# Two gated attention and expert layers: layer 1's values reach their rows through DRAM, probabilities lie by key and then head, layer 0's values are made a step sooner

## The chip, the cores and the metric

One core of a Trainium2 chip runs the whole program. The metric is the time on the device in microseconds; the times are medians of several runs. The engines are PE (TensorE, products and transposes), DVE (VectorE), ACT (ScalarE), POOL (GpSimd) and SP (SyncE, which here only issues transfers). Each engine works through its own list of instructions in order and waits on semaphores.

## What is computed

32 sequences of 128 tokens of width 128, with a context of 77 keys each, go through two layers. Layer 0 attends with 8 heads of 64, layer 1 with 16 heads of 8. After each attention stand 8 experts, of which each token takes two.

```
x = x + tanh(g_xattn[0]) * xattn0(layernorm(x), ctx)      # 8 heads of 64
x = x + tanh(g_ffn[0])   * experts0(layernorm(x))         # top 2 of 8
x = x + tanh(g_xattn[1]) * xattn1(layernorm(x), ctx, ctx) # 16 heads of 8
x = x + tanh(g_ffn[1])   * experts1(layernorm(x))
# xattn1: q = x@Wq+bq; k = ctx@Wk+bk; v = ctx@Wv+bv, by head
#         softmax(q k^T / sqrt(8)) v, then @Wo + bo
```

All of it is float32. Where more accuracy is needed than one rounded product gives, an operand is split into a rounded high part and the rest, and three products are added ("three passes").

## The kernel before

`order` writes out by hand one list of tasks, the plan, by generators for four phases: attention 0 (57 to 278 us of the trace), experts 0, attention 1 (462 to 740 us), experts 1. Every engine walks the same plan and does its part of each task, so the plan sets the order on each queue. A **split task** (`ctx`, `xt`, `q1`, `k1`, `k0` and so on) is a product on PE into a PSUM bank, a rounded copy on ACT and the rest on DVE (L1170, or L1168 with a bias). `bank_of` gives each task its bank. In layer 1 all splits and `v1` use `SPLIT_BANK`, number 5, and so do that layer's routing tasks (`mturn`, `route`, `rank`, `totals`), which pick the experts; a task waits until the one before it in the bank has been read (`bank_free`). Bank 6, `V_BANK`, takes layer 0's values and, in layer 1, the turned values of `rows1`.

Attention works on **units** of 8 heads x 77 keys = 616 columns of scores for 128 tokens. Layer 0 has one unit for a sequence, layer 1 two: 64 units, 8 for a **group** of four sequences. For each unit PE makes the scores (L759, L774), DVE takes the maximum by head (L1154) and subtracts it (L1157) from PSUM into `prob`, ACT takes the exponential, PE turns the 616 columns in five chunks of up to 128 (L782), ACT copies them to `prob_t` (L1082), and PE multiplies them with the values (L801 in layer 0, L816 in layer 1), whose rows must lie as the columns did: by head, then key. In layer 0 DVE also sums each head (L1208) and POOL divides (L1498).

Layer 0's values are made for a sequence in two halves (`v0`, PE L695 to L697, ACT L1069), written to DRAM (SP L624) and read back with the right rows (`v0_load`, SP L630 and L631). They are made in step u for sequence u, loaded in step u + 1, and used by `weigh0` in step u + 2.

Layer 1's values come from `v1`, once for a group: three passes of 308 columns, with the feature on the partition; ACT copies them repeated (L1089, tile `v_t`). `rows1`, twice for each sequence, turns five windows of them on PE (L879, 160 in all), ACT copies these to `v_raw` (L1098, 64 copies), and POOL multiplies with the mask `row_head`, so that each row keeps its own head's 8 columns (L1549, 128 operations, into `v_flat`). Each chunk of `weigh1` reads 108 columns, more than the 72 that it needs. Here the profile writes `v_raw` for `v1_raw`, `v_flat` for `v1_flat` or `v1_rows`, `v_t` for `v1_t`, and `o_both` for `o_sb`.

`up_raw` is the staging tile by which the layer 1 keys and queries go to DRAM (SP L638, L641) and come back stacked (SP L658 with 12 issues for a group, L663).

## Time and profile before

| | us |
|---|---|
| median of 3 runs | 917.65 |
| lowest, highest | 908.68, 921.89 |
| the profiled execution, its own time | 926.61 |
| its span | 924.7 |

| engine | busy us | share of the span |
|---|---|---|
| PE | 725.0 | 78% |
| DVE | 556.2 | 60% |
| POOL | 507.0 | 55% |
| ACT | 458.2 | 50% |

The mean granted TensorE clock is 0.888 of full speed. The span leaves 1.9 us of the profiled time outside, and the profiled execution is 9.0 us longer than the median. Busy shares are means over phases that differ, so each phase has to be read by itself: which engine is nearly full there, and what its idle time waits for.

### The profile page before, as it was taken

To read this page: it belongs to the slowest core of one execution; us is meant where nothing else is said; L and a number is where in the kernel's file an instruction comes from. 1 tells how busy PE (TensorE), PEld (TensorE's weight loads), DVE (VectorE), ACT (ScalarE), POOL (GpSimd) and SP (SyncE) were. 2 spreads that over 40 slices of the span, in tenths; PEclk is the share of its full clock that TensorE was granted. 3 is DMA by queue.
4 is the path that set the end of the run, shared out by engine and by line. 5 is a ranking of instruction groups with operands and counts; after the bars stand their busy time and mean duration, and the time that the engine had idled before them with its cause. 6 is when DMAs were issued, how large, how long until landed. Compare 5 with 4: busy or idle time off the path is not lost.

```text
span 924.7 us, 17016 instructions
## 1 busy us (share of the span) xinstructions
PE 725.0 (78%) x4514; PEld 626.1 (68%) x4514; DVE 556.2 (60%) x1933; ACT 458.2 (50%) x1207; POOL 507.0 (55%) x734
## 2 busy tenths in 40 slices
PE   5677988887879769897867888888788886677870
PEld 3466777777767557786756777777677776676760
DVE  2356777887755546575656767767767634334554
ACT  2355755665534324344455656556466543354441
POOL 4113667675676657556453327547547655655553
PEclk9988997997987979998979989889899977799895
DMA  9225445333342223243523323313313022323444
GB/s 256 100 73 153 144 143 153 117 116 116 115 141 62 72 80 108 73 117 103 150 54 89 99 66 100 99 48 101 113 48 96 30 69 68 95 77 99 127 131 148
DMA packets 131004, 95.91 MB, mean 104 GB/s; under 512 B 30512, under 2 KB 119120, under 8 KB 130848
## 3 DMA queue, kind: packets, MB, share of 16 engines
q1 hardware_dynamic: 118976, 73.89, 29.6%
q0 software_dynamic: 9088, 19.68, 6.0%
q10 hardware_dynamic: 2848, 1.26, 0.5%
q8 instruction: 40, 0.66, 0.3%
q14 instruction: 52, 0.43, 0.2%
HBM read 55.10 MB, written 44.10 MB: 107 GB/s over the span
## 4 chain that ended last, share of the span: by engine, by line
PE 41%; issue 16%; DVE 15%; ACT 10%; POOL 6%; SPq 5%; DMA 4%; another core or an unknown queue 2%; DVEq 0%; POOLq 0%; ACTq 0%
PE banks L816 5%; PE banks L985 5%; POOL y_rows L1594 3%; PE banks L695 3%; PE banks L969 3%; PE banks L960 3%; PE banks L782 2%; PE banks L801 2%; DVE row_max L1154 2%; PE banks L958 2%; PE banks L697 2%; PE banks L959 2%; PE banks L696 2%; PE banks L937 2%
## 5 line engine op out<-in xcount | busy, mean ns | idle before, releaser
L1594 POOL DMA_INDIRECT y_rows<-y_sb,result_at x156 | 151.2, 969 | 128.1 <-DVE y_sb L1408 54.2
L1587 POOL DMA_INDIRECT x_rows<-xm,row x128 | 128.2, 1002 | 40.1 <-issue 30.8
L985 PE MATMUL banks<-down,hidden_t 128*128 x624 | 108.6, 302 | 0.1
L969 PE MATMUL banks<-ident,hidden 128*128 128x128 f32 x312 | 67.1, 300 | 47.9 <-ACT hidden_t L1134 30.3
L1382 DVE TENSOR_TENSOR xb_l<-banks,xb_h 128x128 fp32r<-128x128 f32 x156 | 45.2, 290 | 90.4 <-ACT xb_h L1120 61.1
L816 PE MATMUL banks<-v_flat,prob_t 128*128 128x108 f32 (+2 forms) x640 | 92.6, 298 | 7.0 <-POOL v_flat L1549 5.4
L816 PEld LDWEIGHTS banks<-v_flat,prob_t 128*128 128x128 f32 (+1 forms) x640 | 88.0, 213 | 13.4 <-ACT prob_t L1082 8.2
L1082 ACT ACTIVATE prob_t<-banks 128x512 f32<-128x512 f32 x192 | 73.2, 436 | 41.5 <-PE banks L782 40.6
L985 PEld LDWEIGHTS banks<-down,hidden_t 128*128 128x128 f32 x624 | 92.9, 214 | 0.6 <-issue 0.3
L1549 POOL TENSOR_TENSOR v_flat<-v_raw,row_head 104x64 f32<-104x64 f32 (+1 forms) x128 | 56.2, 464 | 65.2 <-ACT v_raw L1098 64.5
L1154 DVE TENSOR_REDUCE row_max<-banks 128x8 f32<-128x616 f32 x96 | 75.8, 789 | 25.9 <-PE banks L774 19.5
L969 PEld LDWEIGHTS banks<-ident,hidden 128*128 128x128 f32 x312 | 40.6, 150 | 68.3 <-issue 38.0
L1498 POOL TENSOR_TENSOR prob<-prob,inv_sum 128x616 f32<-128x616 f32 x32 | 39.0, 1220 | 58.5 <-DVE inv_sum L1211 58.4
L1134 ACT ACTIVATE hidden_t<-banks 128x256 f32<-128x256 f32 x156 | 59.3, 380 | 20.4 <-remote 10.1
L1126 ACT ACTIVATE gate<-banks 128x256 f32<-128x256 f32 x78 | 29.9, 384 | 79.5 <-PE banks L960 59.6
L1129 ACT ACTIVATE hidden<-banks 128x256 f32<-128x256 f32 x78 | 30.1, 386 | 69.2 <-PE banks L960 40.5
L937 PE MATMUL banks<-ident,x_norm 128*128 128x128 f32 x156 | 48.7, 312 | 18.1 <-DMA x_norm<-x_rows 11.0
L1157 DVE TENSOR_TENSOR prob<-banks,row_max 128x616 f32<-128x616 f32 x75 | 60.0, 800 | 2.6
L801 PE MATMUL banks<-vo_flat,prob_t 128*128 128x128 f32 (+1 forms) x320 | 49.0, 309 | 13.1 <-issue 10.2
L782 PE MATMUL banks<-ident,prob 128*128 128x128 f32 (+1 forms) x375 | 57.5, 288 | 0.0
L1394 DVE TENSOR_TENSOR hidden<-banks,gate 128x256 f32<-128x256 f32 x78 | 32.9, 422 | 40.8 <-ACT gate L1126 22.3
L801 PEld LDWEIGHTS banks<-vo_flat,prob_t 128*128 128x128 f32 (+1 forms) x320 | 46.8, 224 | 14.2 <-issue 11.2
(221 smaller groups left out, 1934.9 us busy)
## 6 DMA issues: line engine op xcount, KB each, us to landing
x_norm<-x_rows SPq DMA_DIRECT2D x156, 72.0 KB
v_rows<-vo SPq DMA_DIRECT2D x64, 154.0 KB
vo_flat<-v_rows SPq DMA_DIRECT2D x32, 256.0 KB
gathered<-y_rows SPq DMA_DIRECT2D x48, 128.0 KB
q_rows<-up_raw SPq DMA_DIRECT2D x8, 512.0 KB
q_even<-q_rows SPq DMA_DIRECT2D x12, 256.0 KB
q_odd<-q_rows SPq DMA_DIRECT2D x12, 256.0 KB
y_rows<-y_sb,result_at POOLq DMA_INDIRECT x156
```

What stands on the lines that cost most here:

```text
L782: done = pe.transpose(banks[0:chunk_rows[c], PT_BANK[k], c % 4 * SEQ:(c % 4 + 1) * SEQ], flat[:, c * P:c * P + chunk_rows[c]], ident[:, :])
L801: done = pe.matmul(banks[:, O_BANK, 0:D], prob_t[0:rows, b % 2, c, :], vo_flat[0:rows, b % 2, c, :], start=c == 0, stop=c == CHUNKS - 1)
L816: done = pe.matmul(banks[:, O_BANK, half * width:half * width + cols], prob_t[0:rows, u % 2, c, :], v1_flat[0:rows, first:first + cols], s ...
L937: pe.transpose(banks[:, X_BANK, 0:P], x_in[:, i % XR, 0:D], ident[:, :]).then_inc(sem("x_turned"))
L969: done = pe.transpose(banks[:, HT_BANK, half * P:(half + 1) * P], hidden[:, i % 2, half * P:(half + 1) * P], ident[:, :])
L985: done = pe.matmul(banks[:, Y_BANK[i % 2], 0:D], hidden_t[:, i % 2, half, :], of_expert(flat[:, (2 * layer + half) * D:], i, D), start=hal ...
L1082: act.activation(dst, banks[0:rows, PT_BANK[k], 0:len(chunks) * SEQ], ACT.Copy).then_inc(sem("prob_t"))
L1134: act.activation(hidden_t[:, i % 2, :, :].rearrange("p t n -> p (t n)"), banks[:, HT_BANK, 0:HID1], ACT.Copy).then_inc(sem("hidden_t"))
L1154: dve.tensor_reduce(m_view, s_view, AX.X, ALU.max).then_inc(sem("row_max"))
L1157: dve.tensor_tensor(prob_view.rearrange("p (k s) n -> p k s n", k=2), s_view, m_view.unsqueeze(3).to_broadcast([P, 2, 4, NKEY]), ALU.subtr ...
L1587: pool.indirect_dma_start(out=x_rows[i // HG][:, :], out_offset=bass.IndirectOffsetOnAxis(ap=row[:, n, c:c + 1], axis=0), in_=xm[:, i % 2, ...
L1594: pool.indirect_dma_start(out=y_rows[k][:, :], out_offset=bass.IndirectOffsetOnAxis(ap=result_at[:, i % (2 * YR):i % (2 * YR) + 1], axis=0 ...
```

## The change

- **Probabilities by key, then head.** `prob` is laid out [77, 8] and no longer [8, 77]. DVE's subtraction reads the scores in PSUM with a step of 77 elements (four heads in the innermost dimension, then the other bank, then the key); the sum by head in layer 0 reads with a step of 8 elements; POOL's division and the exponential read as they lie. A chunk of 128 columns is now 16 keys x 8 heads, except the last, of 13 keys. Layer 0's values are written to DRAM in that order, so a transfer's runs are 2 KB and no longer 512 bytes.
- **Layer 1's values through DRAM.** `v1` has the key on the partition: 4 sequences x three passes of 77 x 128. DVE adds the bias into `up_raw`, after a wait for the keys' transfers out of it; SP writes it to DRAM (`v1_nat`, tile `v_nat` in the rows). A new task `v_load`, for two sequences, reads five chunks back, each key's row repeated on 8 partitions. `rows1` is now POOL alone: two operations of 128 x 320 for a sequence. The mask is the same for all chunks, [128, 8], and is made from the identity by DVE. The 160 transposes, the 64 copies and the repeated copy are gone. `weigh1` reads 72 columns in every chunk.
- **The freed bank.** From group 2 on, `xt`, `k1`, `q1` and `v1` of layer 1 use bank 6; the routing tasks keep bank 5.
- **Layer 0's values a step sooner.** `v0` for sequence u + 1 and `v0_load` for sequence u stand in step u.

```diff
@@ attention0_steps
-        if 0 <= u - 1 < NSEQ:
-            step.append(("v0_load", u - 1))
+        if u == 0:
+            step += [("v0", 0, 0), ("v0", 0, 1)]
         if 0 <= u - 2 < NSEQ:
             step.append(("weigh0", u - 2))
         if u < NSEQ:
-            step += [("v0", u, 0), ("divide0", u)] + more[1]
+            step.append(("v0_load", u))
+        if u + 1 < NSEQ:
+            step.append(("v0", u + 1, 0))
...
@@ attention1_steps
+            if u % 2 == 1:
+                step.append(("rows1", u // 2))
+            if u and u % 4 == 0:
+                step.append(("v_load", u // 4))
@@ prepare_attention1
-    return out + [("norm", n), ("k1", g), ("normalize", n), ("k_load", g), ("xt", n), ("q1", g), ("q_load", g)]
+    out += [("norm", n), ("k1", g), ("normalize", n), ("k_load", g), ("v1", g), ("xt", n), ("q1", g), ("q_load", g)]
+    return out + ([("v_load", 0)] if g == 0 else [])
@@ bank_of
+        if t[0] == "xt" and t[1] >= NG + 2 or t[0] in ("k1", "q1", "v1") and t[1] >= 2:
+            return V_BANK
@@ sync
+                elif t[0] == "v_load":
+                    q = t[1]
+                    w.wait_ge("v1_ones", 6)
+                    w.wait_ge("v1_staged", 16 * (q // 2 + 1))
+                    w.wait_ge("v1", 4 * q)
...
+                    for c in range(CHUNKS):
+                        rows = chunk_rows[c]
+                        sync.dma_start(v1_raw[0:rows, c, :, :].rearrange("p t d -> p (t d)"),
+                                       src[c * KEYS:c * KEYS + rows // UH, :].unsqueeze(1).to_broadcast([rows // UH, UH, 2 * D])).then_inc(sem("v1_in"), 16)
@@ tensor, v1
+                    for j in range(GS):
+                        c0 = g * GK + j * NKEY
+                        done = three_pass(banks[0:NKEY, bank, j * D:(j + 1) * D], ctx_th[:, c0:c0 + NKEY], ctx_tl[:, c0:c0 + NKEY],
+                                          w1_h[:, 2, :], w1_l[:, 2, :])
@@ vector, soften
-                dve.tensor_tensor(prob_view.rearrange("p (k s) n -> p k s n", k=2), s_view,
-                                  m_view.unsqueeze(3).to_broadcast([P, 2, 4, NKEY]), ALU.subtract).then_inc(sem("shifted"))
+                dve.tensor_tensor(prob_view.rearrange("p n (k s) -> p n k s", k=2), s_view.rearrange("p k s n -> p n k s"),
+                                  m_view.unsqueeze(1).to_broadcast([P, NKEY, 2, 4]), ALU.subtract).then_inc(sem("shifted"))
@@ vector, v1
+                    w.wait_ge("k_staged", 16 * HEAD_SETS * (g + 1))
+                    w.wait_ge("q_staged", 16 * g)
+                    dve.tensor_tensor(up_raw[0:NKEY, 0, :].rearrange("n (j d) -> n j d", d=D),
+                                      banks[0:NKEY, bank_of(t), :].rearrange("n (j d) -> n j d", d=D),
+                                      bv1[0:NKEY, :].unsqueeze(1).to_broadcast([NKEY, GS, D]), ALU.add).then_inc(sem("v1_nat"))
@@ gpsimd, rows1
+                    w.wait_ge("v1_in", 16 * CHUNKS * (b // 2 + 1))
+                    w.wait_ge("pv", NSEQ + 2 * (b - 1))
                     for half in (0, 1):
+                        pool.tensor_tensor(v1_rows[:, b % 2, half, :, :, 0:DK1],
+                                           v1_raw[:, :, b % 2 * 2 + half, :].rearrange("p c (h d) -> p c h d", d=DK1),
+                                           row_head[:, :].unsqueeze(1).unsqueeze(3).to_broadcast([P, CHUNKS, UH, DK1]), ALU.mult).then_inc(sem("v1"))
```

PE in attention 1, in the unit in which the routing's `rank` stands (`picked,earlier` to `picked,ones`); `x_norm` is the transpose of `xt`, `v_t` that of `rows1`. Before:

```order
L816 MATMUL banks<-v_flat,prob_t 128x108 x5
L879 MATMUL banks<-ident,v_t 128x128 x4
L782 MATMUL banks<-ident,prob_extra 128x128 x4
L782 MATMUL banks<-ident,prob_extra 104x128
L730 MATMUL banks<-ident,x_norm 128x128 x4
L879 MATMUL banks<-ident,v_t 104x128
L886 MATMUL banks<-ident,o_both 128x128
L920 MATMUL banks<-picked,earlier 128x32
L921 MATMUL banks<-counts,ones 128x32
L923 MATMUL banks<-picked,ones 128x24
```

And in the changed kernel, from the last three of the twelve passes of `v1`:

```order
L722 MATMUL banks<-w_h,ctx_th 77x128
L723 MATMUL banks<-w_h,ctx_tl 77x128
L724 MATMUL banks<-w_l,ctx_th 77x128
L914 MATMUL banks<-ident,o_both 128x128
L948 MATMUL banks<-picked,earlier 128x32
L949 MATMUL banks<-counts,ones 128x32
L951 MATMUL banks<-picked,ones 128x24
L951 MATMUL banks<-picked,ones 128x16
L951 MATMUL banks<-picked,ones 128x8
L807 MATMUL banks<-k_even,q_even 128x308 x2
L848 MATMUL banks<-v_flat,prob_t 128x72 x5
```

Before, `xt` stands ahead of `rank` in bank 5; now `v1` stands there, in bank 6, and `xt` comes a unit later.

SP in attention 1, the transfers of a group. Before:

```order
L658 DMA k_even<-k_rows 8x16x77 [waits k_staged,scores]
L658 DMA k_even<-k_rows 8x16x77 x11
L671 DMA gathered<-y_rows 128x256 [waits combined]
L641 DMA q_rows<-up_raw 128x2x512 [waits q_stack,split_lo]
L663 DMA q_even<-q_rows 32x4x512 [waits q_staged]
L663 DMA q_even<-q_rows 32x4x512 x2
```

In the changed kernel:

```order
L685 DMA k_even<-k_rows 8x16x77 [waits k_staged,scores]
L685 DMA k_even<-k_rows 8x16x77 x11
L658 DMA v_nat<-up_raw 77x512 [waits v1_nat]
L698 DMA gathered<-y_rows 128x256 [waits combined]
L667 DMA v_raw<-v_nat 128x1x256 [waits v1]
L667 DMA v_raw<-v_nat 128x1x256 x3
L667 DMA v_raw<-v_nat 104x1x256
L653 DMA q_rows<-up_raw 128x2x512 [waits q_stack,split_lo]
```

The write of the values and one of the group's two loads (five issues) stand between the keys' loads and the queries' write; the load waits for POOL (`v1`).

PE in attention 0, its first steps: the scores of sequence 0 (`k_t,xt_h`), then keys (`wqk`) and values (`wvo`). Before:

```order
L759 MATMUL banks<-k_t,xt_h 128x308 x4
L759 MATMUL banks<-k_t,xt_l 128x308 x2
L695 MATMUL banks<-ctx_th,wqk_h 128x308
L696 MATMUL banks<-ctx_th,wqk_l 128x308
L697 MATMUL banks<-ctx_tl,wqk_h 128x308
L695 MATMUL banks<-wvo_h,ctx_th 77x512
L696 MATMUL banks<-wvo_h,ctx_tl 77x512
L697 MATMUL banks<-wvo_l,ctx_th 77x512
L695 MATMUL banks<-ctx_th,wqk_h 128x308
```

In the changed kernel:

```order
L792 MATMUL banks<-k_t,xt_l 128x308 x2
L722 MATMUL banks<-ctx_th,wqk_h 128x308
L723 MATMUL banks<-ctx_th,wqk_l 128x308
L724 MATMUL banks<-ctx_tl,wqk_h 128x308
L722 MATMUL banks<-wvo_h,ctx_th 77x512
L723 MATMUL banks<-wvo_h,ctx_tl 77x512
L724 MATMUL banks<-wvo_l,ctx_th 77x512
L722 MATMUL banks<-wvo_h,ctx_th 77x512
L723 MATMUL banks<-wvo_h,ctx_tl 77x512
L724 MATMUL banks<-wvo_l,ctx_th 77x512
L722 MATMUL banks<-wvo_h,ctx_th 77x512
```

Both halves of sequence 0 and the first of sequence 1 now follow the first keys; from there on every pair of halves is one sequence ahead.

## Rows read from the trace of the kernel before

**Rows 1.** The page's first line.

```profile
span 924.7 us, 17016 instructions
```

**Rows 2.** Busy time in three stretches; columns as in its first line.

```profile
core 0: us, PE busy (x) PEld busy (x) DVE busy (x) ACT busy (x) POOL busy (x), PEclk, DMA share, GB/s
57.00:278.00 221.00, 183.25 (x1121) 157.80 (x1121) 159.09 (x509) 124.85 (x276) 135.54 (x178) 0.89 0.45 129
462.00:740.00 278.00, 226.62 (x1564) 201.69 (x1562) 190.46 (x603) 163.54 (x391) 146.05 (x252) 0.90 0.29 79
180.00:210.00 30.00, 24.15 (x165) 20.43 (x163) 25.31 (x87) 18.94 (x42) 20.99 (x29) 1.00 0.41 120
```

**Rows 3.** Waits of PE in 462:740: waited for, us in total, times, longest us.

```profile
PE banks L920 <- DVE xt_l L1170: 10.4, 5, 2.5
PE banks L695 <- ACT v_t L1089: 5.6, 6, 1.1
PE banks L816 <- POOL v_flat L1549: 5.4, 5, 3.0
PE banks L899 <- DVE up_raw L1168: 5.3, 5, 1.1
...
PE banks L879 <- ACT v_raw L1098: 3.0, 4, 1.8
```

**Rows 4.** Timeline, PE: start us, us, engine, line, tiles, count, [idle before <- releaser].

```profile
573.29 1.23 PE L816 MATMUL banks<-v_flat,prob_t 128*128 128x108 f32 x10
...
578.57 0.27 PE L886 MATMUL banks<-ident,o_both 128*128 128x128 f32 x1
581.30 0.26 PE L920 MATMUL banks<-picked,earlier 128*128 128x32 f32 x1 [2.45 <-DVE xt_l L1170]
...
582.60 2.24 PE L816 MATMUL banks<-v_flat,prob_t 128*128 128x108 f32 x10
```

**Rows 5.** Chain of waits, 560:606, in order of time: start us, us, what.

```profile
577.21 0.44 PE banks L879 x4
...
601.54 0.41 PE banks L695
601.95 0.14 PE banks L696
```

**Rows 6.** Groups by line and shape: busy us, mean ns, idle before, releasers.

```profile
L1549 POOL TENSOR_TENSOR v_flat<-v_raw,row_head 128x256 f32<-128x256 f32 x64 | 39.0, 632 | 56.4 <-ACT v_raw L1098 56.1
...
L1549 POOL TENSOR_TENSOR v_flat<-v_raw,row_head 104x64 f32<-104x64 f32 x64 | 17.7, 296 | 8.8 <-ACT v_raw L1098 8.3
...
L1098 ACT ACTIVATE v_raw<-banks 128x512 f32<-128x512 f32 x64 | 28.2, 441 | 45.4 <-PE banks L879 41.0 <-issue 4.3
```

**Rows 7.** DVE by line and shape: busy us, mean ns, idle before, releasers.

```profile
L1157 DVE TENSOR_TENSOR prob<-banks,row_max 128x616 f32<-128x616 f32 x75 | 60.0, 800 | 2.6
...
L1208 DVE TENSOR_REDUCE row_sum<-prob 128x8 f32<-128x616 f32 x32 | 25.4, 792 | 5.2 <-ACT prob L1064 2.4 <-issue 0.5
...
L1170 DVE TENSOR_TENSOR xt_l<-banks,xt_h 128x512 fp32r<-128x512 f32 x16 | 11.0, 690 | 9.6 <-ACT xt_h L1026 8.6 <-issue 1.0
...
L1319 DVE TENSOR_REDUCE row_f<-rank_hot 128x8 f32<-128x64 f32 x16 | 3.5, 220 | 0.5
L1302 DVE TENSOR_REDUCE group_sum<-picked 128x8 f32<-128x32 f32 x16 | 3.4, 209 | 0.5
```

**Rows 8.** Waits of PE in 57:280.

```profile
PE banks L801 <- issue: 10.2, 3, 5.3
...
PE banks L801 <- DMA vo_flat<-v_rows: 2.8, 1, 2.8
```

**Rows 9.** Timeline, 216:232: the load of layer 0's values and its product.

```profile
222.18 0.53 SPq L630 DMA_DIRECT2D vo_flat<-v_rows  x1
...
225.38 1.35 PE L801 MATMUL banks<-vo_flat,prob_t 128*128 128x128 f32 x10 [3.52 <-issue]
```

**Rows 10.** Timeline, SP's queue: the twelve issues of a group's keys.

```profile
571.57 8.33 SPq L658 DMA_DIRECT2D k_even<-k_rows  x12
```

More of the change, by code:

```diff
@@ L51 @@
 CHUNKS = (UNIT_ROWS + P - 1) // P
+FULL = CHUNKS - 1
+KEYS = P // UH
 chunk_rows = [min(P, UNIT_ROWS - c * P) for c in range(CHUNKS)]
-chunk_key = [c * P % NKEY for c in range(CHUNKS)]
 CHUNK_SETS = (range(0, 4), range(4, CHUNKS))
-V1_WINDOW = 108
-REP = max(k + n for k, n in zip(chunk_key, chunk_rows))
-REP_COPIES = (REP + NKEY - 1) // NKEY
 U1 = 2 * NSEQ
@@ L118, in attention0_steps @@
         if u < NSEQ:
-            step += [("v0", u, 0), ("divide0", u)] + more[1]
+            step.append(("v0_load", u))
+        if u + 1 < NSEQ:
+            step.append(("v0", u + 1, 0))
+        if u < NSEQ:
+            step += [("divide0", u)] + more[1]
         if 0 <= u - 1 < NSEQ:
@@ L122, in attention0_steps @@
         if u < NSEQ:
-            step += [("v0", u, 1), ("bias0", u)] + more[2]
+            step += ([("v0", u + 1, 1)] if u + 1 < NSEQ else []) + [("bias0", u)] + more[2]
         step += more[3] + tasks.get(u, [])
@@ L144, in attention1_steps @@
             step.append(("weigh1", u - 3))
-        if u < U1 and u % per == 0:
-            step.append(("v1", u // per))
-        if u < U1 and u % 2:
-            step.append(("rows1", u // 2, 0))
         if 0 <= u - 2 < U1:
@@ L154, in attention1_steps @@
             pending = pending[n:]
-            step.append(("rows1", u // 2, 1) if u % 2 else ("bias1", u // 2))
+            if u % 2 == 0:
+                step.append(("bias1", u // 2))
+            if u % 2 == 1:
+                step.append(("rows1", u // 2))
+            if u and u % 4 == 0:
+                step.append(("v_load", u // 4))
         if 0 <= u - 4 < U1 and u % 2:
@@ L313, in flamingo_two_layers @@
     v_rows = [nc.dram_tensor(f"v_rows{i}", [UNIT_ROWS, D], F32, kind="Internal").ap() for i in (0, 1)]
+    v1_nat = [nc.dram_tensor(f"v1_nat{i}", [NKEY, GS, D], F32, kind="Internal").ap() for i in (0, 1)]
     q_rows = [nc.dram_tensor(f"q_rows{i}", [2, P, GT], F32, kind="Internal").ap() for i in (0, 1)]
@@ L557, in _ @@
                 load(raw1[:, i * D:(i + 1) * D], a[f"L1_xattn_{name}"], "w_layer1")
[L558 to L559 removed]
+            for i, name in enumerate(("bq", "bk")):
+                load(bqk1[:, i:i + 1], a[f"L1_xattn_{name}"].rearrange("(p o) -> p o", o=1), "bqkv1", scattered=True)
+            load(bv1[:, :], a["L1_xattn_bv"].partition_broadcast(P), "bqkv1")
             w.wait_ge("constants", N_CONSTANTS)
@@ L728, in split_task @@
                     w.wait_ge("ln_out", GS * (n + 1))
+                    if bank == V_BANK:
+                        w.wait_ge("y_sb", LAYER_BLOCKS)
                     for j in range(GS):
@@ L745, in split_task @@
                     w.wait_ge("weights1", 6)
+                    if bank == V_BANK:
+                        w.wait_ge("y_sb", LAYER_BLOCKS)
                     done = three_pass(banks[:, bank, 0:GK], w1_h[:, 1, :], w1_l[:, 1, :],
@@ L813, in weigh1 @@
                     rows = chunk_rows[c]
-                    first = ((b % 2 * 2 + half) * CHUNKS + c) * width
-                    cols = width if (half, c) == (1, CHUNKS - 1) else V1_WINDOW
-                    done = pe.matmul(banks[:, O_BANK, half * width:half * width + cols], prob_t[0:rows, u % 2, c, :],
-                                     v1_flat[0:rows, first:first + cols], start=c == 0, stop=c == CHUNKS - 1)
+                    done = pe.matmul(banks[:, O_BANK, half * width:(half + 1) * width], prob_t[0:rows, u % 2, c, :],
+                                     v1_rows[0:rows, b % 2, half, c, :, :].rearrange("p h d -> p (h d)"),
+                                     start=c == 0, stop=c == CHUNKS - 1)
                 done.then_inc(sem("pv"))
@@ L865, in _ @@
                     g = t[1]
[L866 removed]
+                    bank = bank_of(t)
                     w.wait_ge("weights1", 6)
[L868 removed]
+                    w.wait_ge("split_lo", place["ctx", ((g + 1) * GK - 1) // (4 * P)] + 1)
                     w.wait_ge(*bank_free[t])
[L870 to L881 removed]
+                    if bank == V_BANK:
+                        w.wait_ge("y_sb", LAYER_BLOCKS)
+                    for j in range(GS):
+                        c0 = g * GK + j * NKEY
+                        done = three_pass(banks[0:NKEY, bank, j * D:(j + 1) * D], ctx_th[:, c0:c0 + NKEY], ctx_tl[:, c0:c0 + NKEY],
+                                          w1_h[:, 2, :], w1_l[:, 2, :])
+                    done.then_inc(sem("v1_mm"))
                 elif kind == "o_turn":
@@ L981, in _ @@
                         w.wait_ge("o_norm", NSEQ)
-                        w.wait_ge("v1_raw", 2 * NSEQ)
+                        w.wait_ge("split_lo", len(splits))
+                        w.wait_ge("v1_nat", NG)
                     flat = down[:, :, :, :, :].rearrange("p e l t d -> p (e l t d)")
```

116 lines of the change are left out of this document (45 added, 71 removed).

## The prediction

> **What bounds the kernel now.** I read the stretches first. The span is 924.7 us [rows 1]. In attention 1 (462 to 740) PE is busy for 226.6 of 278 us and DVE for 190.5; in attention 0 (57 to 278) they are busy for 183.3 and 159.1 of 221 us [rows 2]. PE is nearest to full in both, but it is not simply full: PE and DVE hand every unit to each other and wait in turn. DVE can be kept fuller than it is: in 180:210 it is busy for 25.31 of 30 us, 84% [rows 2]. I use that share below as the most that DVE reaches here.
>
> Then the waits of PE in attention 1 [rows 3]. The longest are not for the attention's own data but for bank 5: 10.4 us until DVE has read `xt` (PE then does `rank`), 5.6 us until ACT has read `v1`, 5.3 us until DVE has read `k1` (PE then does `mturn`). That is 21.3 us. Another 3.0 us are waits of `rows1` for ACT's copy. The timeline shows one of the long ones: PE stands still for 2.45 us ahead of L920, and then the ten passes of one product with the values take 2.24 us, where they took 1.23 us before the gap [rows 4]: the granted clock has gone from the upper to the lower level, 2.4 to 1.2 GHz. So a gap costs more than its own length.
>
> Last, attention 0: PE waits 10.2 and 2.8 us for its product with the values [rows 8]. In one such place SP issues the load at 222.18, the product starts at 225.38, and PE has been idle for 3.52 us [rows 9]. "issue" hides the transfer, which shares its semaphore with the second load.
>
> **Attention 1, part by part.**
>
> The freed bank removes the 21.3 us of waits for bank 5 from group 2 on, since routing and splits no longer share a bank; in the order of PE `xt` also leaves the unit of `rank`. With them goes at least the clock that the five long gaps cost one product each, 2.24 - 1.23 = 1.0 us: 5 us.
>
> The 160 transposes of `rows1` cost PE 0.44 us for four [rows 5], so 0.11 us each and 17.6 us together, and 3.0 us of waits for ACT go with them. `weigh1` with 72 columns for 108: the five chunks take ten passes of 0.12 us at 108 columns [rows 4], and the 128-column passes of a transpose take the same 0.11, so width is not what they pay for; I take nothing.
>
> `v1` grows from 3 passes of 308 columns to 12 of 128. A pass of 308 columns takes 0.14 us [rows 5]. For 128 columns, below: 0.11, as a transpose, which gives 12 x 0.11 - 3 x 0.14 = 0.9 us for a group. Above: 0.25, as one chunk of the product with the values (1.23 / 5 [rows 4]), which gives 2.6. I take 0.14, since these are rounded operands like the 308-column ones: 1.3 us for a group, 10 us for eight (7 to 21).
>
> PE together: -21.3 - 5 - 17.6 - 3.0 + 10 = -37 us.
>
> ACT loses 64 copies of 28.2 us in all [rows 6] and eight repeated ones; it was not the bound, so that only shortens delays. POOL did 39.0 + 17.7 = 56.7 us of masking in operations of 256 and 64 elements for a partition, 632 and 296 ns [rows 6]; that is 1.75 ns for an element more, so 320 take 744 ns and 64 of them 48 us. Nothing on the path. PE's 5.4 us of waiting for POOL [rows 3] I leave.
>
> DVE gets eight additions of 512 elements: a 512-element operation from PSUM takes 690 ns [rows 7], 5.5 us together. DVE then has 190.5 + 5.5 = 196 us in attention 1, which at 84% needs 233 us. PE's 278 - 37 = 241 is longer, so DVE permits the gain, with only 8 us to spare. I take **-35 us**.
>
> SP gets, for two sequences, five loads, and for a group one write. Twelve issues take 8.33 us [rows 10], 0.69 each, so 3.5 us for five. Behind them stand the queries' write and loads, which have nearly a group to land. In front, a load waits for POOL to finish the odd sequence before. POOL needs the new rows two units later and PE four units later, at 278 / 64 = 4.3 us a unit: 8.7 and 17.4 us. Issue 3.5 plus landing about 3.2 (225.38 - 222.18 [rows 9]) is 6.7. I count nothing; if POOL were late it would show. DVE's new wait for the keys' write stands three units behind `k1`, 13 us: nothing. The first group's transfers fall into experts 0, where 6 x 0.69 = 4 us of SP time could at worst hold up one fetch; I take 0.
>
> **Attention 0.** The load is issued a step (221 / 32 = 6.9 us) sooner, while the waits for it were at most 5.3 us. The 13.0 us go [rows 8], but DVE does part of its other work in these gaps, so half comes back: -6 us (0 to -13).
>
> **The order of the probabilities.** What strided reading costs is the unknown. The nearest row is L1302, which reads 32 elements in SBUF with a step of 8: 209 ns. L1319 reads 64 in sequence in 220 ns [rows 7]. Elements in sequence cost (800 - 690) / (616 - 512) = 1.06 ns each, so 32 of them should take 220 - 34 = 186. The excess of 23 ns is 0.72 ns for an element, if it is by element. For `row_sum` (792 ns) that gives +0.44 us, 32 times: 14 us of DVE in attention 0, or 173 us of 221; at 84% that needs 206. It fits, and I take +2 us.
>
> The subtraction (800 ns, 96 times) has no row like it: its step of 77 elements is in PSUM. Lower bound 0, since one element a cycle may hold whatever the step. A gain is excluded, as no faster row of this kind exists. Nearest row: +0.44. Upper bound: twice the time by element, +0.65. I take 0 as likeliest, but not by much: no PSUM read in these rows shows a cost of the step.
>
> The Trainium skill, Advanced Engine Details and Errata, section Memory Cachelines, speaks against the change: at least two hits on a 16-byte line of SBUF are needed to hide the memory's latency, and PSUM's lines are 8 bytes. By that rule both operations pay, as the rival "strided reads cost" below. The excess at L1302 agrees with it for SBUF; nothing in the rows of before shows it for DVE on PSUM.
>
> **Sum.** -35 - 6 + 2 = -39 us. Against the profiled execution, 926.6 us, that is 887.6, a ratio of 0.958. The profiled execution is 1% above the median of the runs shown; 917.65 x 0.958 = **879 us**, and I say 880.
>
> **The rivals.**
>
> *Strided reads cost, as in L1302 (+0.44 us for each subtraction too).* Attention 1: (196 + 28) / 0.84 = 267 us, so only -11 for -35. Attention 0: (173 + 14) / 0.84 = 223, +2, and the gain of the earlier load is gone. Sum -9: 908 us. For it: L1302. Against: 32 elements are few, and 23 ns can be a fixed cost of another access pattern.
>
> *Strided reads cost double, and it ends slower.* +0.65 us for each: attention 1 (196 + 42) / 0.84 = 283, +5; attention 0 (159.1 + 42) / 0.84 = 239, +18. Sum +23: 940 us. It decides from x us for each of the 128 strided operations where (355 + 128 x) / 0.84 = 499, which is 0.5 us. PE's longer waits would also lower its clock, as in [rows 4], on top. Against: L1302 does not show double (that would be 220 ns).
>
> *The values come late.* One buffer `v1_raw` serves all loads, and if each of the 16 loads kept PE 3 us, that is +48: 927 us, no change. For it: SP's queue has 12 issues of keys in 8.33 us ahead of a load. Against: the 6.7 us against 17.4 worked out above.
>
> *The clock comes back too.* If the gaps' end gives back the clock for the whole unit and not only one product, attention 1 reaches DVE's 233 us, -45, and attention 0 the full -13: sum -56, 862 us.
>
> **Chances.** My forecast 0.48 (865 to 897), the greater gain 0.08, strided reads at a cost between 0.2 and 0.5 us 0.25 (890 to 917), strided reads at double 0.10, late values 0.09. The range takes all but the ends of the first and the last cases: 858 to 926. Faster by over 2% (below 899; a difference of 2% is about what measuring this kernel can tell from none) holds the forecast, the greater gain and a part of the third: 0.63. Slower by over 2% (above 936): 0.10. Within 2%: 0.27.
>
> **What would show each step.** Right: L1157's successor at 800 ns; no wait of PE for bank 5 after 530 us; attention 1 some 35 us shorter at a clock of 0.90 or more; no idle time ahead of layer 0's product with the values; POOL's masking near 744 ns. Wrong: the subtraction at 1.2 us or more and DVE at 84% in both attentions; PE waiting for `v_flat` and POOL for the transfer into `v_raw`; the clock of attention 1 below 0.85, since PE has less to do; passes of 128 columns near 0.25 us.

## The result, and the profile after

| | before | after |
|---|---|---|
| median | 918.44 us | 964.97 us |
| lowest, highest | 908.68, 921.89 | 955.36, 973.00 |

The ratio is 1.049, with a 95% interval of 1.036 to 1.061: the changed kernel is slower. The ratio leaves out the slowest run of the changed kernel, 973.00 us, which ran in a slower state of the chip; the medians as they stand give 1.051. The prediction was 880 us, in a range of 858 to 926. The page of the changed kernel begins with `span 962.4 us`, for the 924.7 us of [rows 1].

Both kernels were profiled once more on one other chip, where the two expert phases are shorter and the attentions hardly differ (861.9 and 897.3 us of span; there the ratio was 1.045, 1.038 to 1.053, over the runs of the changed kernel). Their stretches can be laid side by side. First the kernel before, then the changed one; in each the rows are attention 0, experts 0, attention 1, experts 1, with the start and end, the length, busy time of each engine, TensorE's granted clock (1.00 is 2.4 GHz, and 0.50 is 1.2 GHz), the share of the DMA engines and GB/s.

```profile
core 0: us, PE busy (x) PEld busy (x) DVE busy (x) ACT busy (x) POOL busy (x), PEclk, DMA share, GB/s
38.50:278.50 240.00, 196.64 (x1184) 166.64 (x1182) 169.48 (x536) 134.82 (x298) 140.96 (x188) 0.90 0.43 123
278.50:443.50 165.00, 148.89 (x896) 126.50 (x895) 108.08 (x431) 72.62 (x248) 110.47 (x129) 0.93 0.37 107
443.50:713.60 270.10, 223.57 (x1557) 199.59 (x1557) 186.49 (x582) 161.15 (x388) 145.35 (x252) 0.91 0.29 80
713.60:861.90 148.30, 108.99 (x807) 98.48 (x806) 78.48 (x360) 75.91 (x254) 98.90 (x113) 0.88 0.43 128
```

```profile
38.70:283.80 245.10, 197.08 (x1184) 166.03 (x1182) 194.39 (x536) 135.47 (x298) 148.41 (x186) 0.91 0.40 120
283.80:452.60 168.80, 151.35 (x907) 128.35 (x907) 108.16 (x432) 72.56 (x248) 112.64 (x132) 0.93 0.39 111
452.60:746.80 294.20, 227.29 (x1458) 212.71 (x1457) 193.93 (x589) 134.46 (x316) 135.04 (x188) 0.79 0.39 109
746.80:897.30 150.50, 109.40 (x807) 98.65 (x806) 79.00 (x360) 76.29 (x254) 99.43 (x113) 0.88 0.43 127
```

Attention 1 is 24.1 us longer where 35 less were forecast, attention 0 5.1 us longer where 4 less were forecast, and experts 0 3.8 us longer. In attention 1 the clock fell from 0.91 to 0.79: PE has 99 instructions fewer and is still busy for longer. DVE's busy time rose by 7.4 us there (5.5 were forecast) and by 24.9 us in attention 0 (14 were forecast).

What the operations of the changed kernel cost, from its first trace; the columns are those of [rows 6] and [rows 7].

```profile
L1171 DVE TENSOR_TENSOR prob<-banks,row_max 128x616 f32<-128x616 f32 x75 | 60.0, 800 | 2.6
...
L1517 POOL TENSOR_TENSOR prob<-prob,inv_sum 128x616 f32<-128x616 f32 x32 | 48.1, 1504 | 61.9 <-DVE inv_sum L1238 61.8
L1567 POOL TENSOR_TENSOR v_flat<-v_raw,row_head 128x320 f32<-128x320 f32 x64 | 46.4, 747 | 85.8 <-DMA v_raw<-v_nat 72.3 <-PE banks L848 13.3
...
L1235 DVE TENSOR_REDUCE row_sum<-prob 128x8 f32<-128x616 f32 x32 | 42.3, 1321 | 5.6 <-ACT prob L1094 2.5 <-issue 0.5
```

The subtraction still takes 800 ns. The sum of a row went from 792 to 1321 ns. POOL's division, 1220 ns in the kernel before, takes 1504. The mask takes 747 ns.

The row sum is 17 us of the 24.9 that DVE gained in attention 0. Most of the rest is in small operations that read only SBUF: on the chip of the rows above, `shift_n` went from 420 to 1217 ns (7 times) and `rank_hot` from 234 to 770 ns (6 times), together 8.8 us. A timeline of the changed kernel there shows one of this kind, `picked`, which starts just behind POOL's division and ends with it:

```profile
150.48 1.47 POOL L1517 TENSOR_TENSOR prob<-prob,inv_sum 128x616 f32<-128x616 f32 x1
150.60 1.40 DVE L1326 TENSOR_TENSOR picked<-hot 128x32 fp32r<-128x32 f32 x1
```

It takes 394 ns on average in that attention. No run tests whether POOL's work is the cause.

What PE waits for in attention 1 (474 to 782 us of the same trace), as in [rows 3]:

```profile
PE banks L848 <- POOL v_flat L1567: 18.1, 7, 3.5
PE banks L807 <- DVE prob L1171: 12.8, 11, 2.7
PE banks L807 <- DMA q_odd<-q_rows: 11.4, 4, 4.4
PE banks L807 <- DMA q_even<-q_rows: 7.3, 3, 3.1
PE banks L807 <- DVE prob_extra L1171: 4.5, 5, 1.3
PE banks L848 <- issue: 3.2, 1, 3.2
```

The waits for bank 5 are gone. In their place stand waits for POOL's masked values, for the queries' loads and for DVE's `prob`. Timelines show how both loads come late: PE first (the view ends at 600 us, so its last row has seven of the ten passes), then POOL, then SP's queue.

```profile
583.92 0.88 PE L807 MATMUL banks<-k_odd,q_odd 96*128 96x308 f32 x2 [1.98 <-DMA q_odd<-q_rows]
584.60 2.25 PE L848 MATMUL banks<-v_flat,prob_t 128*128 128x72 f32 x10
...
593.79 1.23 PE L848 MATMUL banks<-v_flat,prob_t 128*128 128x72 f32 x10
...
598.52 1.74 PE L848 MATMUL banks<-v_flat,prob_t 128*128 128x72 f32 x7 [2.19 <-POOL v_flat L1567]
```

```profile
583.09 1.43 POOL L1567 TENSOR_TENSOR v_flat<-v_raw,row_head 128x320 f32<-128x320 f32 x2
...
596.85 1.58 POOL L1567 TENSOR_TENSOR v_flat<-v_raw,row_head 128x320 f32<-128x320 f32 x2 [9.37 <-DMA v_raw<-v_nat]
```

```profile
575.10 0.39 SPq L653 DMA_DIRECT2D q_rows<-up_raw  x1
...
578.16 1.28 SPq L690 DMA_DIRECT2D q_odd<-q_rows  x3
...
589.84 1.72 SPq L650 DMA_DIRECT2D k_rows<-up_raw  x4
591.66 3.36 SPq L667 DMA_DIRECT2D v_raw<-v_nat  x5
```

POOL is done with the old rows at 584.5, so the next value load could go then. It goes at 591.66: in SP's queue it stands behind the keys' write, which waits for DVE's split of `k1`. In the second trace of this kernel a value load directly follows the keys' write in six of the seven groups. POOL gets the rows at 596.85 and PE its values at 598.52. The queries' write goes at 575.10 and their loads at 578.16; PE needs them a unit later and waits. After the gaps ten passes take 2.25 us, the lower level of 1.2 GHz, where they take 1.23 at the upper one.

### The profile page after: what moved, and what is told of

Its sections match the earlier page's. It is cut to its first block, busy times and chain, and to the rows that moved or that the text cites. A ratio compares the mean times of both kernels' runs of the same rounds, so it can differ in the third digit from the quotient of the medians.

```text
span 962.4 us, 16767 instructions
## 1 busy us (share of the span) xinstructions
PE 747.2 (78%) x4426; PEld 652.3 (68%) x4426; DVE 588.0 (61%) x1942; ACT 432.2 (45%) x1135; POOL 506.1 (53%) x668
## 4 chain that ended last, share of the span: by engine, by line
PE 33%; DVE 17%; issue 13%; POOL 11%; DMA 10%; ACT 6%; SPq 6%; another core or an unknown queue 3%; POOLq 0%; DVEq 0%; ACTq 0%
POOL y_rows L1613 7%; PE banks L848 6%; PE banks L816 4%; PE banks L1014 3%; PE banks L722 2%; DMA q_rows<-up_raw 2%; DVE row_sum L1235 2%; DVE row_max L1168 2%; PE banks L988 2%; DMA q_odd<-q_rows 2%; PE banks L997 2%; SPq L667 2%; DVE prob L1171 2%; PE banks L724 2%
## 5 line engine op out<-in xcount | busy, mean ns | idle before, releaser
L1606 POOL DMA_INDIRECT x_rows<-xm,row x128 | 128.2, 1002 | 36.5 <-issue 30.6
L848 PE MATMUL banks<-v_flat,prob_t 128*128 128x72 f32 (+1 forms) x640 | 109.2, 335 | 22.2 <-POOL v_flat L1567 18.1
L848 PEld LDWEIGHTS banks<-v_flat,prob_t 128*128 128x128 f32 (+1 forms) x640 | 107.1, 253 | 26.8 <-issue 24.7
L1567 POOL TENSOR_TENSOR v_flat<-v_raw,row_head 128x320 f32<-128x320 f32 x64 | 46.4, 747 | 85.8 <-DMA v_raw<-v_nat 72.3
L1517 POOL TENSOR_TENSOR prob<-prob,inv_sum 128x616 f32<-128x616 f32 x32 | 48.1, 1504 | 61.9 <-DVE inv_sum L1238 61.8
L816 PE MATMUL banks<-ident,prob 128*128 128x128 f32 (+1 forms) x375 | 67.1, 321 | 0.0
L816 PEld LDWEIGHTS banks<-ident,prob 128*128 128x128 f32 (+1 forms) x375 | 54.9, 174 | 1.1 <-POOL prob L1517 0.2
L722 PE MATMUL banks<-ctx_th,wqk_h 128*128 128x308 f32 x64 | 27.0, 422 | 34.1 <-DVE k_t L1187 30.2
```

What stands on the lines that cost most here:

```text
L816: done = pe.transpose(banks[0:chunk_rows[c], PT_BANK[k], c % 4 * SEQ:(c % 4 + 1) * SEQ], flat[:, c * P:c * P + chunk_rows[c]], ident[:, :])
L848: done = pe.matmul(banks[:, O_BANK, half * width:(half + 1) * width], prob_t[0:rows, u % 2, c, :], v1_rows[0:rows, b % 2, half, c, :, :].r ...
L1517: pool.tensor_tensor(pv, pv, inv_sum[:, b % 2, 0:UH].unsqueeze(1).to_broadcast([P, NKEY, UH]), ALU.mult).then_inc(sem("divided"))
L1606: pool.indirect_dma_start(out=x_rows[i // HG][:, :], out_offset=bass.IndirectOffsetOnAxis(ap=row[:, n, c:c + 1], axis=0), in_=xm[:, i % 2, ...
```

## Experiments

Ratios are to the kernel before on the same chip. Each set of runs was made on one chip, and the chips are of two kinds: "fast" ones with experts 1 near 149 us, and ones like that of the first traces, with 182 to 192. Three chips are fast: that of the two tables of rows above (it also ran the section on columns and late loads), that of the four single steps, and that of the steps on the mended kernel. Stretches are compared within one kind, but often between two chips, and each is from one profiled execution. One kernel that was profiled twice on one chip had 233.6 and 236.4 us in attention 0 and 265.4 and 269.0 in attention 1, so a difference of 3 to 4 us in a stretch shows nothing by itself.

### Four single steps on the changed kernel

108 columns in the product of layer 1's values:

```diff
-  done = pe.matmul(banks[:, O_BANK, half * width:(half + 1) * width], ..., v1_rows[0:rows, b % 2, half, c, :, :]...)
+  first = ((b % 2 * 2 + half) * CHUNKS + c) * width
+  cols = width if (half, c) == (1, CHUNKS - 1) else 108
+  done = pe.matmul(banks[:, O_BANK, half * width:half * width + cols], ..., v1_flat[0:rows, first:first + cols], ...)
```

> The changed kernel, but each chunk of weigh1 again reads 108 columns for its 72. Two theories of the clock in attention 1, which fell from 0.90 to 0.74: (B) the narrower products leave PE too little to do, then 108 columns bring the clock above 0.85 and attention 1 from 308 us back by 20 us or more, the whole to 0.98 to 1.02 of before; (A) PE waits for late query rows and masked values, and the clock falls in those gaps: then 108 columns change nothing, clock 0.74 to 0.78 and 1.04 to 1.06 of before.

Ratio 1.041 (1.031 to 1.051), fast chip. Attention 1, whose row stands below with others, takes 286.6 us at a clock of 0.86, 7.6 us less than the changed kernel at 0.79. That is the clock of theory B with nearly the time of theory A. The totals are too close to tell apart: 1.041 for 1.045, and the intervals overlap.

The values' task in the unit of `k_load`, so that the queries come a unit sooner:

```diff
+            if pending and pending[0][0] == "k_load":
+                n = 2
             step += pending[:n]
```

> The changed kernel, but v1 stands in the same unit as k_load, so that q1 and q_load come one unit sooner, as before the change. PE waited 39.7 us for the loads of the query rows. (A) These waits are the cause: they fall below 10 us, attention 1 comes down by 25 to 40 us with a clock above 0.80, and the whole is at 1.00 to 1.02 of before. (B) If the narrow products set the clock, only part of the waits comes back: 10 us or less, 1.035 to 1.05 of before, clock below 0.78.

Ratio 1.050 (1.041 to 1.059), attention 1 293.7 us at a clock of 0.77: nothing. (The 39.7 us of the expectation counted the waits of products and of weight loads together; PE's products waited 18.7 us, as in the rows above.) PE's waits for the queries are gone, and these stand in their place, in attention 1:

```profile
PE banks L850 <- issue: 26.7, 11, 3.2
PE banks L809 <- DVE prob L1173: 13.6, 11, 3.0
PE banks L809 <- DVE prob_extra L1173: 10.4, 5, 5.8
PE banks L850 <- POOL v_flat L1569: 5.3, 2, 3.4
```

The product with the values (L850) now waits instead: with one late load mended the other is late.

Layer 0's probabilities by head, then key, as before the change, with the division, the row sum and the write of the values that belong to it; its values are still made a step sooner:

```diff
-  soften(b, b, prob[:, b % 2, :, :], 2 * (b - 1))
+  soften(b, b, head_major(b), 2 * (b - 1), True)    # [8, 77] in place of [77, 8]
```

> The changed kernel, but layer 0's probabilities lie by head, then key, and its values in DRAM too; layer 1 as changed. DVE's sum by head should go from 1321 back to 792 ns and POOL's division from 1504 to 1220 ns, 17 us of DVE and 9 us of POOL. If attention 0 is bound by DVE, it shortens from 226 by 10 to 15 us to below before's 221, since the values come a step sooner: 1.03 to 1.04 of before. If this lies under other work, below 3 us: 1.045 to 1.05.

Ratio 1.029 (1.020 to 1.039). Attention 0 takes 233.8 us, for 245.1 in the changed kernel and 240.0 in the kernel before. So the order by key costs attention 0 11.3 us, and the earlier values give 6.2.

Layer 1's splits in bank 5 again:

```diff
-        if t[0] == "xt" and t[1] >= NG + 2 or t[0] in ("k1", "q1", "v1") and t[1] >= 2:
-            return V_BANK
```

> The changed kernel, but layer 1's splits and v1 stay in bank 5 with the routing. My prediction gave the freed bank 26 us. If that holds also here, this is slower than the changed kernel by 15 to 30 us, 1.065 to 1.08 of before. If the late loads stand last anyway, or the new order (xt a unit behind rank) does it without the other bank, by less than 5 us: 1.045 to 1.055.

Ratio 1.063 (1.054 to 1.072), attention 1 307.7 us: 13.5 more than the changed kernel.

### Do columns set the clock, and do late loads set the time?

The two kernels again, for the two tables of rows in the section on the result:

> The kernel before once more, unchanged, for a trace from the same chip as the three below. Every theory expects a ratio of 1.00, with attention 1 near 250 us at a clock of 0.90 if this chip is one of the faster ones, where experts 1 took 149 us in the last four runs, and 274 us at 0.90 if it is like the first.

> The changed kernel once more, for a trace beside the kernel before on one chip. Expected 1.05 (1.04 to 1.06). The attention stages together should be longer by 35 to 45 us: 10 us in attention 0, 30 in attention 1.

The kernel before with 72 columns for 108:

```diff
-  cols = width if (half, c) == (1, CHUNKS - 1) else V1_WINDOW
+  cols = width
```

> The kernel before with one edit: its product of layer 1's values takes 72 columns in every chunk in place of 108, which is all that the output needs (the extra ones are zero products). Nothing else moves. Theory 'fewer columns cost clock': the clock of attention 1 falls below 0.85 (from 0.90) and the kernel is slower, by 5 to 15 us, ratio 1.005 to 1.015. Theory 'gaps alone cost clock' (the changed kernel's clock fell because PE waited longer for queries and values, and the columns have no part in it): clock 0.90, ratio 0.99 to 1.00, since each of 640 passes gets shorter or stays.

The median was 871.6 us for 858.4 (4 runs from 862.8 to 877.7, too scattered for an interval). Its profile, of 866.0 us, has attention 1 at 269.2 us and a clock of 0.90, as before (270.1, 0.91), so that stretch shows no cost of the narrow passes. But the clocks over the whole program were 0.905, 0.906, 0.887 and 0.886, for 0.915 to 0.925 in the seven runs of the kernel before on this chip, and the two quicker runs, 862.8 and 866.0 us, lie at the slow end of those seven (857.0 to 863.5) or above it. Whether narrow passes cost this kernel some us is open.

108 columns, the queries sooner, and the value loads queued at the end of the unit before:

```diff
-            if u and u % 4 == 0:
-                step.append(("v_load", u // 4))
+            if u % 4 == 3 and u < U1 - 1:
+                step.append(("v_load", u // 4 + 1))
```

> The changed kernel with three edits: 108 columns in the product of layer 1's values, the v1 task in the unit of k_load (so that queries are made a unit sooner), and the loads of the value rows queued at the end of the unit before instead of the middle of the next. Theory 'late loads': with the waits for queries (about 21 us) and for values (26 us, or PE's 27 us put down to issue once the queries were sooner) both gone, attention 1 comes down by 25 us or more from the 287 us of the run with 108 columns, and the ratio to 1.015 or less; what remains over the kernel before lies in attention 0. Theory 'DVE and clock': the loads are late only because units are long; the waits move to DVE's prob, and attention 1 stays above 280 us, ratio 1.035 to 1.045.

Ratio 1.028 (1.021 to 1.034): between the two theories. Attention 1 of the run with 108 columns, and of this one:

```profile
456.70:743.30 286.60, 212.11 (x1456) 196.96 (x1456) 192.34 (x589) 133.72 (x316) 135.60 (x188) 0.86 0.40 112
```

```profile
456.10:730.20 274.10, 206.86 (x1457) 191.69 (x1457) 194.25 (x589) 132.79 (x316) 135.62 (x188) 0.87 0.41 117
```

Mending the late loads was worth 12.5 us of attention 1 by these profiles, and 11 us by the ratios (1.041 to 1.028). But PE now waits 30.5 us for `prob`, and DVE and ACT wait for transfers out of one staging tile:

```profile
PE banks L809 <- DVE prob L1174: 18.7, 15, 3.3
PE banks L809 <- DVE prob_extra L1174: 11.8, 8, 5.0
```

```profile
DVE up_raw L1199 <- DMA k_rows<-up_raw: 11.7, 5, 3.0
```

```profile
ACT up_raw L1057 <- DMA v_nat<-up_raw: 10.2, 4, 4.2
```

### A staging tile of its own

The same, with the values staged in the idle `gate` tile from group 1 on:

```diff
+        def v1_stage(g):
+            return up_raw[0:NKEY, 0, :] if g == 0 else gate[0:NKEY, :, :].rearrange("n a b -> n (a b)")
```

> The run without late loads (1.028) with one more edit: from group 1 on the values are staged in a buffer of their own (the gate buffer of experts 0, idle by then) and not in up_raw, which the keys' and the queries' splits use too. Theory 'one staging buffer chains three steps': DVE's 11.7 us of waits for the keys' write (5 times, up to 3.0) and ACT's 10.2 us for the values' write go, DVE's subtraction comes sooner, and PE's 30.5 us of waits for prob and prob_extra fall below 20; attention 1 at 262 to 268 us for 274, ratio 1.012 to 1.020. Theory 'DVE is the bound': DVE only waits elsewhere, attention 1 stays within 3 us of 274, ratio 1.025 to 1.030.

Ratio 1.021 (1.013 to 1.029), on a chip of the slower kind. Attention 1 took 265.3 us there, where the first trace of the kernel before has 273.7, and the waits for `prob` fell from 30.5 to 24.0 us. The ratio came down by 0.007, some 6 us, and the intervals overlap: the direction is that of the first theory, the size is loose. Layer 0 by head on top of it, called the mended kernel from here:

> The same with layer 0's probabilities by head, then key, as before, but its values still a step sooner. If the costs add up, attention 0 falls from 246 to 234 us as it did in the run of layer 0 by head, and the ratio is 0.013 below that of the run with its own stage: 1.00 to 1.007 by the first theory there, 1.012 to 1.017 by the second. Below 0.99 only if the order of the probabilities also costs something in attention 1.

Ratio 1.003 (0.998 to 1.008), and measured again 1.002 (0.998 to 1.006):

> The run with its own stage and layer 0 by head once more, unchanged, as the base of the four runs that changed one thing in it. From those: attention 0 at 234 to 236 us, attention 1 at 265 (clock 0.88), ratio 1.000 to 1.005.

So the mends together take away the whole loss, and of the gain that was forecast there is none in the total. The profile of that run has attention 0 at 236.4 us and attention 1 at 269.0, where the first trace of before, on a chip of that kind, has 239.2 and 273.7. Both attentions are shorter than before, but experts 0 takes 193.6 us for 184.1 (189.6 in the first profile of this kernel) and eats that up.

### One step each on the mended kernel (fast chip)

Only the row sum of layer 0 with a step of 8:

```diff
-  dve.tensor_reduce(row_sum[:, b % 2, :], head_major(b), AX.X, ALU.add)
+  dve.tensor_reduce(row_sum[:, b % 2, :], prob[:, b % 2, :, :].rearrange("p n h -> p h n"), AX.X, ALU.add)
```

> The run with its own stage and layer 0 by head, with one edit: DVE's row_sum reads its 616 elements with a step of 8, as in the changed kernel, though they lie by head; so it adds the wrong elements, and layer 0's result is wrong. Division, transposes and transfers stay as they were. 32 operations should take 1321 ns for 792, 17 us of DVE. If DVE's sum is the whole cost of the order by key in layer 0, attention 0 goes from 234 to 245 us and the ratio from 1.003 to 1.015. If the division on GpSimd (1504 ns for 1220) and the write of the values carry most of it, attention 0 stays below 238 us.

Ratio 1.011 (1.003 to 1.019). Attention 0 and attention 1:

```profile
38.70:284.50 245.80, 200.25 (x1185) 169.24 (x1183) 190.19 (x537) 135.23 (x298) 138.53 (x185) 0.89 0.42 119
456.00:720.70 264.70, 201.14 (x1458) 187.06 (x1457) 194.70 (x589) 133.01 (x316) 136.26 (x188) 0.89 0.43 122
```

The first row is as long as that of the changed kernel (245.1), with the division at its old 1217 ns. The three other kernels by head on this chip had attention 0 at 235.5 to 236.6 us, so the sum alone costs 9 to 10 us, which is nearly all of the 11.3. The second row is the mended attention 1 on a fast chip and the base of the next three runs.

72 columns:

> The run with its own stage and layer 0 by head, with 72 columns in the product of layer 1's values for 108. Theory 'gaps alone cost clock': attention 1 stays within 3 us of 265 and its clock within 0.02 of 0.86 to 0.88, as the same edit in the kernel before did nothing. Theory 'columns cost clock where PE has gaps': the clock falls below 0.83 and attention 1 takes 272 us or more, as the first of these runs had it the other way round (0.79 to 0.86, 294 to 287 us).

Ratio 1.012 (1.004 to 1.020):

```profile
445.60:724.10 278.50, 217.63 (x1458) 204.94 (x1457) 194.65 (x590) 133.36 (x316) 136.79 (x188) 0.80 0.41 116
```

The clock fell from 0.89 to 0.80. This profile is of the slowest of six runs (876.8 us, median 870.3), so some 6 of its 13.8 us are of that run. By medians the step costs about 10 us, since 869.95 of the run above holds 10 us in attention 0 that this kernel hasn't. The clock doesn't hang on that one profile: over the whole program the other five runs had 0.881 to 0.891, those of the run above 0.901 to 0.910. So narrow passes do cost clock in this kernel, as in the changed one.

Splits in bank 5:

> The run with its own stage and layer 0 by head, with layer 1's splits back in bank 5. The prediction had 21.3 us of waits for that bank and 5 us of clock. If the freed bank is worth that, attention 1 takes 285 us or more for 265, ratio 1.025. If its waits only stand where others would (PE would wait for prob or the queries there), half or less: 268 to 275 us, ratio 1.007 to 1.014.

Ratio 1.011 (1.002 to 1.019), attention 1 272.4 us for 264.7: the bank is worth 7.7 us here, for 13.5 in the changed kernel, though its waits are back nearly in full:

```profile
PE banks L952 <- DVE xt_l L1196: 13.0, 5, 3.4
```

```profile
PE banks L931 <- DVE up_raw L1194: 5.2, 5, 1.2
```

Every second value load behind the queries' write:

> The run with its own stage and layer 0 by head, with every second value load (the one of a group's second pair) queued behind the queries' write and not ahead of it. If the value loads in SP's queue make the queries late, PE's 17 us of waits for q_even and q_odd fall below 6 and attention 1 to 260 us or less, ratio 0.993 to 0.999. If they only trade places, waits for v_flat and issue rise from 10 us to 20 or more and the ratio stays at 1.00 to 1.01.

Ratio 1.004 (0.999 to 1.008). The waits for queries are gone (20.2 us in the base), those for `v_flat` and issue are 35.0 us for 12.2, and attention 1 takes 271.6 (the profiled execution, 869.4 us, is 6.5 above the median): they trade places.

144 columns, on the other kind of chip:

> The mended kernel with 144 columns for 108 in the product of layer 1's values (the output needs 72; the others are computed and not used). Theory 'columns hold the clock where PE has gaps': the clock of attention 1 rises from 0.88 to 0.90 or more and attention 1 falls by 2 to 6 us. Theory 'full already': the clock stays, and each of 640 passes costs the same or some ns more; attention 1 stays or grows by up to 3 us.

Ratio 1.003 (1.000 to 1.006). The clock of attention 1 rose to 0.90, for 0.86 and 0.87 in the two profiles with 108, and the stretch took 267.6 us for 265.4 and 269.0: more clock and no less time.

### The earlier values alone, on the kernel before

> The kernel before with one part of the change alone: layer 0's values are made a step sooner and their load is queued a step sooner. Probabilities, layer 1 and banks stay. If the earlier load is worth what the prediction said (-6 us), attention 0 takes 234 us for 240 and the ratio is 0.993 (0.988 to 0.997). If PE only stands idle elsewhere in the step, 1.00. If it is more than 1.00, the earlier products delay the keys' splits on DVE and ACT.

> The kernel before with only layer 0's values a step sooner, once more with five rounds. Expected 0.993 to 0.998: attention 0 4 to 6 us shorter than the 240 us that this kind of chip had before.

Ratios 0.997 (0.992 to 1.001) and 1.001 (0.997 to 1.004). Attention 0 took 235.6 and 233.8 us, for 239.2 in the first trace of before; but experts 0 took 188.3 and 187.7 us for 184.1. In the total there is nothing that can be measured. No kernel here beat the kernel before.

## Why the prediction was wrong, step by step

Attention 1 was forecast 35 us shorter and came 24.1 us longer. Of these 59 us, the runs put 29.5 on three costs that the sum set at nothing (the late loads, the shared staging tile, the narrow passes), and 29.6 on the worth of the work removed from PE, which was taken in full. "Slower by over 2%" had a chance of 0.10, and for another mechanism, strided reads at double cost, which did not happen. Two of the prediction's own signs of being wrong did come: PE waiting for `v_flat` and POOL for the transfer into `v_raw`, and a clock of attention 1 below 0.85.

**"I count nothing" for SP's queue and the late values: failed.** This is the first of the large errors. Two things were overlooked. The list of a group's tasks grew from seven to eight, which put the queries a unit later, so "nearly a group to land" was not there. And the estimate of 6.7 us against 17.4 began at the issue; it left out what stands ahead of `v_load` in SP's queue, the keys' write that waits for DVE, which the trace after shows as 7.1 us (584.5 to 591.66). Mending both was worth 12.5 us, and mending the queries alone nothing. The rival "the values come late" had the mechanism, at 0.09, but set against it the full gain of 39 us and so expected no change.

**"DVE's new wait for the keys' write [...]: nothing": failed once the rest was mended.** `up_raw` is one tile for keys, values and queries. Its own tile took attention 1 from 274.1 to 264.7 us, 9.4 us; these are profiles of two fast chips, and by the ratios it is some 6. It holds for the kernel with the `v1` task next to `k_load`; how much of it the changed kernel pays, where these stand a unit apart, wasn't run.

**The clock: wrong sign and size.** The forecast gave back 5 us of clock with the gaps. The clock of attention 1 fell from 0.91 to 0.79 instead. Most of that is the narrow passes, not the gaps: with 108 columns and every late load still in place it is 0.86, and mending the loads brings only 0.87. So the term "I take nothing" for 72 columns failed: 108 gave back 7.6 us (profiles of two fast chips), and in the mended kernel the step is worth about 10. "Width is not what they pay for" holds for the length of a pass at one clock, and leaves out what the passes do to the clock. The three steps, 7.6 + 12.5 + 9.4 = 29.5 us, lead from 294.2 to 264.7.

**"PE together -37 us": the removed work was right, its worth was not.** With all three mended, PE is busy for 201.1 us for 223.6, 22.4 less, yet attention 1 is only 5.4 us shorter (264.7 for 270.1). PE is idle for 63.6 us where it was for 46.5. The bank's 21.3 + 5 us were worth 13.5 in the changed kernel and 7.7 in the mended one. The sum took PE's busy time and PE's waits as if PE alone set the length. PE, DVE, POOL and the loads hand each unit on in turn; the time that PE no longer needed became a wait for `prob` (23.7 us for 6.4 before) and for queries (20.2 for 3.6). "233 us" as the bound by DVE at 84% wasn't reached: DVE was busy for 194.7 of 264.7, 74%. The 84% came from one stretch of 30 us, in attention 0.

**The row sum: direction right, mis-sized.** 529 ns for an operation where 440 were forecast, 17 us of DVE; and attention 0 paid 11.3 for the new order, 9 to 10 of them for the row sum, where 2 were taken. "It fits" under 84% was the wrong test. The row sum stands ahead of `k_t` in DVE's order, and PE waits for `k_t`: 24.2 us at L722 in the changed kernel and 18.6 with layer 0 by head, for 16.5 before, all on fast chips. With the other places where PE waits for `k_t` the new order adds 7.1 us of such waits (30.6 for 23.5); the other 4 of the 11.3 are busy time of PE (197.1 for 193.1).

**The subtraction: right.** 800 ns with a step of 77 elements in PSUM. The Trainium skill, Advanced Engine Details and Errata, section Memory Cachelines, asks for at least two hits on a line of SBUF and for PSUM that every two consecutive elements be contiguous, and the prediction read this as a cost of both operations. For SBUF the row sum agrees with it (792 to 1321 ns with a step of 32 bytes); for a tensor_tensor operation of DVE that reads PSUM the measurement differs, and it decides. What the section says is slowed there are matmuls. The two operations differ in kind, memory and step at once, and no run separates these. That the prediction took 0, "but not by much", was a guess that came out.

**The earlier load: right in its stretch.** -6.2 us in attention 0 (layer 0 by head against the kernel before), -3.6 and -5.4 in the two profiles of the edit alone, for -6; the product's waits of 10.2 and 2.8 us [rows 8] are gone. Alone it brings nothing to the total, though. Experts 0 is 3.6 to 4.2 us longer in the two profiles of that edit alone; why, no run tells.

**Right too:** the mask (747 ns for 744), the five issues of a value load (3.36 us for 3.5) and the passes of `v1`, which start 0.13 us apart where 0.14 was taken:

```profile
602.00 0.33 PE L724 MATMUL banks<-w_l,ctx_th 128*77 128x128 f32 x1
602.13 0.33 PE L722 MATMUL banks<-w_h,ctx_th 128*77 128x128 f32 x1
```

**What stays open:** why experts 0 is longer in the changed kernel and in all that have the earlier values. On fast chips it takes 168.8 to 171.5 us for 165.0; on the others 187.7 to 193.6 for 184.1. On fast chips the mended kernel gains some 4 us in attention 0 and 5.4 in attention 1, and loses 5 to 6 of these 9 in experts 0. Open is also whether two buffers for the value rows, which would free the loads from POOL, make the rest worth its while. They don't fit into SBUF as the kernel lays it out, and it wasn't tried.

## What to carry to other kernels

Before a transfer is called hidden, walk the issuing queue from the moment its data is ready: what stands ahead of it, and which engine does that wait for. In a list of tasks dealt out one to a unit, a task that is added moves all behind it by a unit. Where engines hand each unit on in a ring, busy time taken from one of them is worth a fraction (here 5 us of 22), while time added to an operation that another engine waits behind costs most of itself (here 9 to 10 of 17). And a stretch that gets shorter is worth only what the total shows: here the phase behind it got longer.

## What the hardware showed unexpectedly

- A DVE reduction of 616 elements that reads SBUF with a step of 8 elements takes 1321 ns for 792, but a subtraction that reads PSUM with a step of 77 takes the same 800 ns as one in sequence.
- POOL's multiplication of 616 elements takes 1504 ns for 1217 when `inv_sum` is repeated over the outer dimension (77 times 8 values) and not the inner one (each of 8 values 77 times), though the large operand lies in sequence in both.
- Useless columns can pay: 108 for 72 raised the granted clock of attention 1 from 0.79 to 0.86 and took 7.6 us off, and in the mended kernel it made 0.89 of 0.80 and was worth about 10 us. In the kernel before the same step left that stretch as it was (0.91 for 0.90), and 144 for 108 raised the clock by 0.03 and brought nothing that can be measured.
